# Ten slots instead of eight for gathered rows in a decoder layer, paid for with halved row buffers

## The reference

```python
x = _layernorm(x + _L0_attn_ref(x, ...))
# cross-attention: each row attends to itself and to 12 nodes of a tree
nk = flatK[:, :, idx_table]                     # 12 gathered key rows per query row
nv = flatV[:, :, idx_table]
nbr_logits = jnp.einsum('bhld,bhlnd->bhln', Q, nk) * scale
w = jax.nn.softmax(all_logits, axis=-1)         # 13 logits: self and 12 nodes
out = jnp.einsum('bhln,bhlnd->bhld', w, all_v) @ Wo.T + bo
x = _layernorm(x + out)
h = jax.nn.relu(x @ w1 + b1);  x = _layernorm(x + h @ w2 + b2)
```

## Time and profile before

| | us |
|---|---|
| Time, median of 3 runs (lowest, highest) | 2362.91 (2362.0, 2380.96) |
| Profiled execution, its time | 2362.72 |
| Its span in the profile | 2360.7 |
| Stage 1, about | 0 to 1125 |
| Stage 2, first transpose of tile 2 to that of tile 31 | 1264.53 to 2280.28 |
| Rest, PE and ACT alone | 2280.28 to 2360.7 |

### The profile page before, as it was taken

How to read it: one execution, slowest core, us unless ns; L and a number is a source line. 1 busy time by engine, 2 the same in 40 slices (tenths; PEclk the granted TensorE clock), 3 DMA queues, 4 the chain that set the end, 5 groups by cost and what they waited for, 6 DMA issues and landing times.

```text
span 2360.7 us, 33037 instructions
## 1 busy us (share of the span) xinstructions
PE 2049.5 (87%) x11360; PEld 1023.6 (43%) x11360; DVE 1616.1 (68%) x2129; ACT 1072.2 (45%) x1854; POOL 1036.9 (44%) x1084
## 2 busy tenths in 40 slices
PE   4899999999999999996147888998989999988997
PEld 2333333333333333331014555555555555555555
DVE  8564647566564647552568888888888888888850
ACT  3354545455555545464013444444444444444444
POOL 3232534244352535233444464465555555455420
PEclk9999999999999999998568999999999999999999
DMA  5442434434342434331875675665665675675520
GB/s 193 146 126 73 144 97 131 145 108 152 121 149 79 142 96 130 117 108 63 311 268 186 220 235 188 220 231 199 221 236 195 215 255 195 206 249 195 199 85 18
DMA packets 188800, 392.40 MB, mean 166 GB/s; under 512 B 20692, under 2 KB 82260, under 8 KB 188632
## 3 DMA queue, kind: packets, MB, share of 16 engines
q1 hardware_dynamic: 133336, 188.91, 25.1%
q0 software_dynamic: 55296, 201.35, 24.6%
HBM read 312.33 MB, written 77.59 MB: 165 GB/s over the span
## 4 chain that ended last, share of the span: by engine, by line
DVE 28%; DMA 11%; POOL 5%; issue 4%; PE 3%; ACT 0%; DVEq 0%; SPq 0%; ACTq 0%; POOLq 0%
DMA nb<-kv_flat,idx_rows 10%; DVE bank L1497 10%; DVE logits L1444 5%; POOL nb L1568 5%; DVE nb L1493 5%; DVE nb L1435 4%; PE bank L1172 1%; PE bank L1148 1%; DMA own<-kv_flat 1%; DVE bank L1503 1%; DVE logits L1448 1%; DVE own L1439 1%; DVE total L1474 1%; DVE top L1466 1%; DVE weights L1481 0%
## 5 line engine op out<-in xcount | busy, mean ns | idle before, releaser
L712 DVE TENSOR_REDUCE neg_max<-rows_ps 128x2 f32<-128x1024 f32 x256 | 312.4, 1220 | 298.3 <-PE rows_ps L499 298.2
L1568 POOL DMA_INDIRECT nb<-kv_flat,idx_rows x384 | 366.6, 955 | 138.0 <-issue 86.2
L1435 DVE TENSOR_TENSOR nb<-nb,bank 128x1024 f32<-128x1024 f32 x192 | 231.7, 1218 | 142.5 <-DMA nb<-kv_flat,idx_rows 137.7
L627 ACT ACTIVATE probsT<-e_ps 128x1024 f32<-128x1024 f32 x256 | 262.0, 1023 | 145.1 <-PE e_ps L527 144.8
L1596 POOL TENSOR_TENSOR nb<-nb,weights 128x1024 f32<-128x1024 f32 x96 | 182.5, 1914 | 281.8 <-DVE weights L1481 281.1
L1497 DVE TENSOR_TENSOR bank<-bank,nb 128x512 f32<-128x512 f32 x384 | 268.2, 698 | 24.7 <-DVE bank L1497 0.5
L1148 PE MATMUL bank<-x2T_hi,w_hi_sb 128*128 128x256 f16 x1024 | 282.4, 276 | 0.7 <-issue 0.7
L1148 PE MATMUL bank<-x2T_lo,w_hi_sb 128*128 128x256 f16 x1024 | 281.9, 275 | 0.0
L1148 PE MATMUL bank<-x2T_hi,w_lo_sb 128*128 128x256 f16 x1024 | 281.4, 275 | 0.0
L517 PE MATMUL o_ps<-probsT,v_sb 128*33 128x512 f32 x1024 | 269.6, 605 | 6.3 <-ACT oT L624 6.1
L1444 DVE TENSOR_REDUCE logits<-nb 128x32 f32<-128x1024 f32 x192 | 230.0, 1211 | 0.0
(11 more groups left out here) (158 smaller groups left out, 3611.8 us busy)
## 6 DMA issues: line engine op xcount, KB each, us to landing
kv_flat<-kv_nat SPq DMA_DIRECT2D x128, 256.0 KB, 3.3
own<-kv_flat SPq DMA_DIRECT2D x32, 512.0 KB, 3.8
q_stack<-qk_dram SPq DMA_DIRECT2D x96, 128.0 KB, 3.0
k_stack<-qk_dram SPq DMA_DIRECT2D x96, 128.0 KB, 3.3
piece<-in_pieces SPq DMA_DIRECT2D x40, 256.0 KB, 3.5
in_sb<-in_xT SPq DMA_DIRECT2D x8, 1024.0 KB, 6.6
in_sb<-in_ctxT SPq DMA_DIRECT2D x8, 1024.0 KB, 5.6
qk_dram<-hi SPq DMA_DIRECT2D x32, 256.0 KB, 2.2
```

Source lines behind the costliest of these rows:

```text
L627: act.activation(probsT[:, (d - E_LAG) % TT, :, :], e_ps[:], ACT.Exp, scale=1.0 / (Q_UP * K_UP))\
L712: dve.tensor_reduce(neg_max[:, g % 2, at:at + 2], rows_ps[:], AX.X, ALU.max, negate=True).then_inc(max_done, 1)
L1435: dve.tensor_tensor(kk, kk, q.unsqueeze(1).to_broadcast([P, GN, D]), ALU.mult)\
L1568: pool.indirect_dma_start(nb[:, slot(lt, g), k, :], None, kv_flat, bass.IndirectOffsetOnAxis(idx_rows[:, lt, at:at + 1], 0))\
```

## The change

- `SLOTS` goes from 8 to 10. `AHEAD` follows: four groups of the next tile instead of two. `KEYS_AHEAD` stays 2. As 24 groups per batch are no multiple of 10, `slot` and `fills` now count over all batches.
- `o_sb` and `x2` hold one tile, `squares` one each for x2 and y, `y_sb` one round of two tiles. So `copy_acc` now waits for the stores of the round just before, and `y_square` of the second tile waits for the first.
- To make that possible, SP's stores stand in the middle of `round_moves`, after the load of `own` for the next round's first tile and before the second `x1_in` load.
- The bias buffers of the start lie over `y_sb` and the x2 transposes.

```diff
-SLOTS = 8
+SLOTS = 10
-            o_sb = sb("o_sb", [P, 2, D])
+            o_sb = sb("o_sb", [P, D])
-            x2 = sb("x2", [P, 2, D])
-            squares = sb("squares", [P, 1 + RT, D], F16)
-            y_sb = sb("y_sb", [P, TT, D])
+            x2 = sb("x2", [P, D])
+            squares = sb("squares", [P, 2, D], F16)
+            y_sb = sb("y_sb", [P, RT, D])
+            bias_in, bias_hi, bias_lo = y_sb[0:2], x2T_hi[0:2, 0:2, :], x2T_lo[0:2, 0:2, :]
-            def slot(lt, g):
-                return (lt * NG + g) % SLOTS
+            def slot(b, lt, g):
+                return ((b * TT + lt) * NG + g) % SLOTS
             def fills(b, lt, g):
-                return b * (TT * NG // SLOTS) + (lt * NG + g) // SLOTS + 1
+                return ((b * TT + lt) * NG + g) // SLOTS + 1
...
                     if ahead > 0:
                         load_own(nb_, nh * RT)
+                    if not (isinstance(b, int) and b * 2 + half < 2):
+                        store(b - 1, half)
                     if ahead > 1:
                         load_x1(fb, fh * RT + 1)
                     if ahead > 0:
                         load_res(nb_, nh * RT)
                         load_own(nb_, nh * RT + 1)
-                    if not (isinstance(b, int) and b * 2 + half < 2):
-                        store(b - 1, half)
...
                 def copy_acc(b, half):
                     act.wait_ge(mlp_ready, START + b * 2 + half + 1)
-                    act.wait_ge(out_stored[half], START + b * (16 * RT))
+                    pb, ph = last_round(b, half)
+                    if b * 2 + half:
+                        act.wait_ge(out_stored[ph], START + (pb + 1) * (16 * RT))
...
                 def y_square(b, half):
                     act.wait_ge(y_centre, START + b * 2 + half + 1)
-                    act.wait_ge(y_squared, START + (b * 2 + half) * RT)
                     for lt in tiles(half):
                         s = 2 + lt % 2
+                        act.wait_ge(y_squared, START + (b * 2 + half) * RT + lt % RT)
```

More of the change, by code:

```diff
@@ L1024, in store @@
                         sp.dma_start(out[bass.ds(b, 1), lt * P:(lt + 1) * P, :].rearrange("a p d -> p (a d)"),
-                                     y_sb[:, lt, :]).then_inc(out_stored[half], 16)
+                                     y_sb[:, lt % RT, :]).then_inc(out_stored[half], 16)
                 def round_moves(b, half, ahead):
@@ L1113, in turn_out @@
                     pe.wait_ge(o_copied, START + b * TT + lt + 1)
-                    turn(turn_of(b, lt, "o"), o_sb[:, lt % 2, :])
+                    turn(turn_of(b, lt, "o"), o_sb[:])
                 def turn_query(b, lt):
@@ L1282, in copy_o @@
                     act.wait_ge(o_part, START + (b * TT + lt + 1) * O_STEPS)
-                    act.activation(o_sb[:, lt % 2, :], O[:], ACT.Copy).then_inc(o_copied, 1)
+                    act.activation(o_sb[:], O[:], ACT.Copy).then_inc(o_copied, 1)
                 def exponentials(b, lt):
@@ L1304, in x2_square @@
                     act.wait_ge(x2_squared, START + n)
-                    act.activation(squares[:, 0, :], x2[:, s, :], ACT.Square, bias=neg_mean[:, s:s + 1],
+                    act.activation(squares[:, 0, :], x2[:], ACT.Square, bias=neg_mean[:, s:s + 1],
                                    accum_out=sum_squares[:, s:s + 1]).then_inc(x2_squared, 1)
@@ L1326, in y_square @@
                     act.wait_ge(y_centre, START + b * 2 + half + 1)
-                    act.wait_ge(y_squared, START + (b * 2 + half) * RT)
                     for lt in tiles(half):
                         s = 2 + lt % 2
-                        act.activation(squares[:, 1 + lt % RT, :], y_sb[:, lt, :], ACT.Square, bias=neg_mean[:, s:s + 1],
+                        act.wait_ge(y_squared, START + (b * 2 + half) * RT + lt % RT)
+                        act.activation(squares[:, 1, :], y_sb[:, lt % RT, :], ACT.Square, bias=neg_mean[:, s:s + 1],
                                        accum_out=sum_squares[:, s:s + 1]).then_inc(y_squared, 1)
@@ L1336, in y_apply @@
                         s = 2 + lt % 2
-                        act.activation(y_sb[:, lt, :], y_sb[:, lt, :], ACT.Identity, scale=rstd[:, s:s + 1],
+                        act.activation(y_sb[:, lt % RT, :], y_sb[:, lt % RT, :], ACT.Identity, scale=rstd[:, s:s + 1],
                                        bias=shift_by[:, s:s + 1]).then_inc(y_ready, 1)
@@ L1432, in multiply @@
                         if g < NG:
-                            dve.wait_ge(gathered[slot(lt, g)], (16 * GN) * fills(b, lt, g))
-                            kk = nb[:, slot(lt, g), :, 0:D]
+                            dve.wait_ge(gathered[slot(b, lt, g)], (16 * GN) * fills(b, lt, g))
+                            kk = nb[:, slot(b, lt, g), :, 0:D]
                             dve.tensor_tensor(kk, kk, q.unsqueeze(1).to_broadcast([P, GN, D]), ALU.mult)\
@@ L1489, in multiply @@
                     def multiply(g):
-                        dve.wait_ge(gathered[slot(lt, g)], (16 * GN) * fills(b, lt, g))
-                        vv = nb[:, slot(lt, g), :, D:2 * D].rearrange("p n (h d) -> p n h d", h=H)
+                        dve.wait_ge(gathered[slot(b, lt, g)], (16 * GN) * fills(b, lt, g))
+                        vv = nb[:, slot(b, lt, g), :, D:2 * D].rearrange("p n (h d) -> p n h d", h=H)
                         w = w_ps[:, g * GN:(g + 1) * GN, :].unsqueeze(3).to_broadcast([P, GN, H, DH])
@@ L1567, in gather @@
                         at = g * GN + k
-                        pool.indirect_dma_start(nb[:, slot(lt, g), k, :], None, kv_flat,
+                        pool.indirect_dma_start(nb[:, slot(b, lt, g), k, :], None, kv_flat,
                                                 bass.IndirectOffsetOnAxis(idx_rows[:, lt, at:at + 1], 0))\
-                            .then_inc(gathered[slot(lt, g)], 16)
+                            .then_inc(gathered[slot(b, lt, g)], 16)
                 def summed(b, i):
```

29 lines of the change are left out of this document (13 added, 16 removed).

## The result

The changed kernel was slower: 2430.02 us median (2425.57 to 2434.09) against 2362.45 (2355.44 to 2380.96), a ratio of 1.0273 with a 95% interval of 1.021 to 1.0336. 2263 had been forecast.

The account below looks back on a forecast made before the run. DVE was taken to set the pace while waiting for gathers. Fourteen rounds going from 70.33 to 63.33 us save 98.0, the last tile 3, the start costs 1: 100 less, forecast 2263 us, range 2247 to 2292.

Parts of the forecast that it names:

- PE's side of a round: Stage 2: PE's work over a round of two tiles, put at 62.85 to 63.6 us.
- the query loop: Stage 2: DVE waits 1.7 us for PE's query each round; the loop through both engines takes 63.33 us.
- the one on the slow side (SP's stores): Rival, chance 0.02: SP's stores wait for `y_apply` and delay later loads, 8 us a round; 2384 us.
- DVE's waits for gathers go: Stage 2: ten slots remove all DVE waits for gathered rows, 34.76 - 3.96 = 30.80 us a tile.
- gathers still late: Rival, chance 0.17: group 5 costs 1.5 us in both tiles, 21 us over 14 rounds; 2284 us.
- group 5: Sixth key group of a tile, wanted 5.7 us after DVE's last addition; expected in time by 0.3 to 1.6 us.
- Clock: PE's clock in stage 2: low-clock stretches cost 2.1 us a round before; none counted with waits of half a microsecond.
- Other edits at nothing: Halved `y_sb`, `o_sb`, `x2`, `squares`, moved stores and bias staging cost nothing; `squares` 3 us if its cover is gone.
- Start: Before the second tile: four more gathers delay `own` by 5.2 us, recovered waits give back 4.3; net +1, -4 to +6.
- Sum: Whole kernel: 98.0 us from 14 rounds, 3 from the last tile, plus 1 at the start: 100 less, 2262.7 us.

Follow-up runs that it names:

- chip 8: Changed kernel, unchanged, run again on this chip: 2258.67 us, ratio 0.9572; the kernel before took 2359.92 there.
- chip 4: Changed kernel with eight slots again, all other edits kept, run on this chip: 2361.14 us, ratio 1.0001 against the kernel before.
- the paced kernel: Changed kernel with POOL filling an unused 128x512 buffer ahead of each gather of a burst but the first four: 2260.41 us, elsewhere 2258.34.
- chip 13: Changed kernel with multiply and reduce in turn 2433.72 us, DVE awaiting the next gather 2429.25, pauses between gathers 2260.41; kernel before with half rows 2402.54.
- the first eight runs: Four runs on chip 4, then four on chip 13: seven variants of the changed kernel, one of the kernel before; 2255.69 to 2433.72 us.
- the two unpaced kernels on chip 13: Changed kernel with DVE multiplying and reducing in strict turn, 2433.72 us; changed kernel with DVE waiting for the next group's gather, 2429.25 us.

## Why the prediction was wrong

It was wrong by 167 us and in sign. The step that failed is "PE's side of a round", 62.85 to 63.6 us, and with it the query loop of 63.33: both took from the trace of before, without saying so, that a signal of PE arrives at once (12.8 to the end of the query's last matmul, 12.9 "with the signal"). In the measured execution signals of PE came up to 9.3 us after their matmul's start, 97 of them in stage 2, and a round took 74.8 us, of which PE was idle for 10.1. These rounds are 14 x 11.5 = 161 us of the 167. No rival had this; the one on the slow side (SP's stores) didn't occur: DVE has no wait for `own` in the rounds. By the steps:

- *DVE's waits for gathers go.* Right, on both kinds of chip: 125.4 us to none.
- *The rival "gathers still late".* It had 2284 and did not occur: with ten slots group 5 was in time. Nine slots, where DVE still waits 37.4 us for rows, took 2280; that the two numbers are close is chance.
- *The loop.* On chip 8 each piece was there. DVE's timeline:

```profile
1894.48 2.34 DVE L1435 TENSOR_TENSOR nb<-nb,bank 128x1024 f32<-128x1024 f32 x2
...
1908.07 2.35 DVE L1435 TENSOR_TENSOR nb<-nb,bank 128x1024 f32<-128x1024 f32 x2 [1.94 <-PE bank L1106]
...
1926.93 2.34 DVE L1435 TENSOR_TENSOR nb<-nb,bank 128x1024 f32<-128x1024 f32 x2
...
1957.35 2.34 DVE L1435 TENSOR_TENSOR nb<-nb,bank 128x1024 f32<-128x1024 f32 x2
```

  The wait for the query is 1.94 us (1.7 forecast), from there 18.86 to the end of the tile (18.85), and 30.42 for the next (30.80). The steady round is 62.88 (63.33). The 0.4 too many lie in the tile of before that was read: where DVE waits, its next instruction doesn't overlap the last one by the usual 0.08 us, and one pause of 0.12 us is too short to be marked; neither counts as idle time in the row.
- *Clock.* No loss with short waits: 1.00 on chip 8. In the measured execution it was 0.94, where PE had waits of up to 5.9 us; the forecast had counted none of this, as its waits were to be short.
- *Other edits at nothing.* Right on chip 4: 1.0001 (0.999 to 1.0011) for all of them together.
- *Start.* On chip 8 `own` was there 27.5 us after the first copy of `o_sb` (1183.21), in place of 22.8 (1184.43): 4.7 later, forecast 5.2. DVE waits 19.6 us for it, and not 9.03 + 5.2, as its gather waits ahead of it are gone. The transpose of tile 2 came at 1264.40 against 1264.53: net 0, forecast +1.
- *Sum.* 2258.67 us on chip 8, 4 less than the 2263 of the forecast, mostly from the 0.4 above; the mechanism was right there. In the first measurement it was 2430.

My chance of 0.95 was held against mechanisms within the kernel. It left no room for something outside it that the one trace did not show: before's came from an execution with its signals in time.

## What to carry to other kernels

When waits are taken away, the kernel leans on signals being prompt. Waits marked "remote" on a single core were, in all four traces that had them, signals that came late; missing records alone were no proof, as the paced kernel on chip 13 lost them too and had its signals in time. Repeat an unchanged kernel on another chip before looking for the cause in its text: the first eight runs, split over two chips, had pointed to the bytes, and it was not them. Where GpSimd issues many gathers in a row and nothing waits for the last of them, a pause of half a microsecond between them cost nothing where signals were prompt (2258.34 against 2258.67) and was worth 170 us where they weren't (2260.41 against 2430); the paced kernel is the version to keep. These two pairs differ in kind: the first ran on one chip, the second compares chip 13 with the first measurement; against the two unpaced kernels on chip 13 itself the pause was worth 169 and 173 us.

## What the runs showed of the hardware that I had not expected

- In five executions, on chip 13 and in the first measurement, GpSimd issued gathers 1.24 us apart and signals of PE came up to 10.4 us after their matmul's start, most of them as an issue ended or 2.0 to 2.4 us after the burst's last one. In the fifth, the paced kernel, it was one signal, in the burst without pauses; at 1.65 us apart there was none. DVE's and ACT's recorded signals were in time, but for one of ACT in one run (2.7 us). On three other chips of four no signal was late; the unchanged kernel with ten slots ran on one of these.
- The effect did not shrink with the bytes: with half rows and eight slots 111 signals of PE were late, and ACT waited up to 6.2 us.
- Late signals left PE waits of up to 5.9 us, and its granted clock over 28 tiles was 0.94 in place of 1.00: 115.6 us at the lower of its two levels in place of 3.4. PE was busy 45.9 us longer, more than a quarter of the loss.
